# A gated attention and ternary feed-forward block: other places for evictions, and a reordered start-up

## What is computed

```python
x = x + tanh(g_xattn[0]) * attention(layernorm(x), ctx_768, Wq, Wk, Wv, Wo, bo)   # softmax(q k^T / 8) v, then @ Wo + bo
x = x + tanh(g_ffn[0]) * ffn(layernorm(x), w_gate, w_up, w_down)
# ffn: every product is act_quant(h) @ weight_quant(w).T
#   act_quant: rows rounded to 127 steps of their largest magnitude
#   weight_quant: round(w / mean|w|) clipped to -1, 0, 1, times mean|w|
#   h = square(relu(h @ w_gate.T)) * (h @ w_up.T), then @ w_down.T
```

## Time and profile before

| | |
|---|---|
| median of 3 runs | 1192.87 us (1192.4 to 1193.15) |
| the profiled execution | 1192.44 us |
| its span | 1190.6 us |
| TensorE busy | 1170.7 us (98%) |
| VectorE busy | 1034.7 us (87%) |
| ScalarE busy | 870.4 us (73%) |
| GpSimd busy | 300.1 us (25%) |
| mean granted TensorE clock | 0.997 |

### The profile page before, as it was taken

One profiled execution on the slowest core, in us unless ns is written; L12 is line 12 of the kernel. 1 busy time (PEld: TensorE's weight loads), 2 busy tenths in 40 slices (PEclk: granted clock), 3 DMA queues, 4 the chain that ended last, 5 costly groups with the idle time before them and its releaser, 6 DMA issues.

```text
span 1190.6 us, 18823 instructions
## 1 busy us (share of the span) xinstructions
PE 1170.7 (98%) x5851; PEld 740.8 (62%) x5851; DVE 1034.7 (87%) x2124; ACT 870.4 (73%) x929; POOL 300.1 (25%) x301
## 2 busy tenths in 40 slices
PE   9979999999999999999999999999999999999998
PEld 7546656666665666566566656666665666566554
DVE  4988898888988888888998888889899888988887
ACT  5877777776887777677877767776787777677764
POOL 3121222222442222222442222222244222222200
PEclk9999999999999999999999999999999999999999
DMA  9873554443444464444444464443444444444333
GB/s 375 279 255 81 149 145 108 98 110 92 100 115 101 118 164 112 97 106 101 101 99 101 114 172 115 97 110 93 101 112 102 99 97 113 98 105 100 87 66 71
DMA packets 289780, 144.69 MB, mean 122 GB/s; under 512 B 254651, under 2 KB 258063, under 8 KB 287569
## 3 DMA queue, kind: packets, MB, share of 16 engines
q1 hardware_dynamic: 289741, 144.32, 47.4%
q10 hardware_dynamic: 4, 0.00, 0.0%
HBM read 57.86 MB, written 24.35 MB: 69 GB/s over the span
## 4 chain that ended last, share of the span: by engine, by line
PE 87%; DVE 4%; DMA 3%; ACT 2%; SPq 2%; issue 2%; POOL 0%; DVEq 0%; ACTq 0%
PE gu_ps L1110 34%; PE o_ps L1074 18%; PE y_ps L1124 17%; PE s_ps L68 17%; DMA staged<-in_wg_t 2%; SPq L522 1%; DVE half_max L1365 1%; DVE staged L1359 1%; DMA a_scr<-a_spare 1%; DMA hq_t<-staged 0%; PE gu_ps L1243 0%; ACT staged L800 0%; DVE pt_low L1348 0%; PE gu_ps L1212 0%; DVE prob_sum L1341 0%
## 5 line engine op out<-in xcount | busy, mean ns | idle before, releaser
L1110 PE MATMUL gu_ps<-w_up,xq_t 128*128 128x512 bf16 x1024 | 241.9, 379 | 1.9 <-DVE staged L1359 1.8
L1110 PE MATMUL gu_ps<-w_gate,xq_t 128*128 128x512 bf16 x1016 | 240.9, 380 | 1.5 <-DMA xq_t<-xq 1.0
L1124 PE MATMUL y_ps<-w_down,hq_t 128*128 128x512 bf16 x1008 | 228.0, 379 | 0.5 <-DMA hq_t<-staged 0.5
L1074 PE MATMUL o_ps<-v_sb,pt_high 128*128 128x512 f32 (+1 forms) x640 | 214.7, 416 | 6.3 <-DVE pt_low L1348 6.3
L1359 DVE TENSOR_TENSOR staged<-staged,gu_ps 128x1024 f32<-128x1024 f32 x128 | 155.6, 1215 | 54.2 <-ACT staged L806 54.2
L68 PE MATMUL s_ps<-a_sb,xf_high 128*128 128x308 f32 x1024 | 187.4, 305 | 0.0
L1110 PEld LDWEIGHTS gu_ps<-w_up,xq_t 128*128 128x128 bf16 x1024 | 99.8, 98 | 123.8 <-DVE staged L1359 3.8
L846 ACT ACTIVATE staged<-staged,h_scale 128x1024 f32<-128x1024 f32 x126 | 137.9, 1142 | 48.5 <-DVE h_scale L1379 48.5
L1124 PEld LDWEIGHTS y_ps<-w_down,hq_t 128*128 128x128 bf16 x1008 | 98.7, 98 | 119.6 <-DMA hq_t<-staged 1.0
L670 POOL TENSOR_TENSOR rstd<-var_eps,neg_half 128x1 f32<-128x1 f32 x128 | 95.8, 748 | 304.5 <-DVE var_eps L1324 275.6
L800 ACT ACTIVATE staged<-gu_ps 128x1024 f32<-128x1024 f32 x127 | 129.1, 1016 | 52.1 <-PE gu_ps L1110 52.0
(11 more groups left out here) (155 smaller groups left out, 1421.0 us busy)
## 6 DMA issues: line engine op xcount, KB each, us to landing
xf_sb<-in_x_feat SPq DMA_DIRECT2D x64, 256.0 KB, 2.6
x_sb<-in_x_tok SPq DMA_DIRECT2D x64, 256.0 KB, 2.8
y<-staged SPq DMA_DIRECT2D x63, 256.0 KB, 2.1
staged<-in_wg_t SPq DMA_DIRECT2D x4, 1024.0 KB, 18.1
folded<-a_scr SPq DMA_DIRECT2D x3, 1232.0 KB, 6.2
staged<-in_wd_t SPq DMA_DIRECT2D x3, 1024.0 KB, 8.5
folded<-v_scr SPq DMA_DIRECT2D x3, 1024.0 KB, 5.7
w_up<-in_wu_t SPq DMA_DIRECT2D x2, 1024.0 KB, 16.2
```

What stands on the lines that cost most here:

```text
L1074: last = nc.tensor.matmul(o_ps[:, :], pt[0:rows, P * c:P * (c + 1)], v_sb[0:rows, v, c, :], start=(c == 0 and pt is pt_high and v == 0), s ...
L1110: last = nc.tensor.matmul(target[:, q, :], xq_t[:, s.par(0), c, :], w[:, c, cols], start=(c == 0), stop=(c == DC - 1))
L1124: last = nc.tensor.matmul(y_ps[:, :], hq_t[:, c, :], w_down[:, c, :], start=(c == 0), stop=(c == FC - 1))
```

## The change

**Places.** `bo_sb` becomes a buffer of 128 partitions instead of one. The five places of the later values are rows of `x1` (0 to 2), `bo_sb` (3), and the first 512 floats of each partition of `planes_t` (4); all are contiguous rows of 512 floats, and `k_pairs` isn't used for it any more. Parts 0 to 9 go to k mod 5, parts 10 to 15 to places 0, 1, 2, 3, 0, 1. A part waits for the one that had its place: part 14 for part 10, part 15 for part 11. The first turning of planes (tile 1's) waits until place 4 has been stored.

**SyncE's list.** `turn_probs(start, 1)` and `store_keys(3, 2)` go ahead of `store_later_values(11)` and `(12)`.

**ScalarE's list.** `part_probs(start, 1)` goes ahead of `measure(2, 1)`; `measure(2, 3)` leaves ScalarE; `exponentials(start, 2)` goes behind the join and high part of tile 1.

**VectorE's list.** `sum_probs(start, 1)` goes ahead of `ternary(1, 2, w_up)`; `measure(2, 3)` comes in behind `measure(2, 2)`; `probs_low(start, 1)` goes between the two scales; `sum_probs(start, 2)` goes behind `ternary(2, 1, w_down)`; `ternary(2, 0, w_down)` goes into step 0, behind `shift_scores` of tile 3, and there `hidden_half(s, 1)` and `probs_low(s, 2)` go ahead of `top_half(s, 0)` and `ternary(2, 2, w_down)`.

```diff
@@ -39,7 +39,8 @@
 PIECE = WEIGHT // PIECES
 PARTS = PIECE // 512
 A_RING = 2
-V_OUT_RING = 5
+V_PLACES = 5
+V_PLACE = [k % V_PLACES if k < 2 * V_PLACES else (k - 2 * V_PLACES) % (V_PLACES - 1) for k in range(16)]
 FIRST_ROWS = ((BATCH - 1) * KEYS + 1) // 2
 V_LATER = 2 * HEADS
 V_RING = 2
@@ -175,7 +176,7 @@
         v_t = sb("v_t", [P, HP, BATCH * KEYS], F32)
         v_pairs = sb("v_pairs", [P, HP, ALL_KEYS], F32)
         ones = sb("ones", [P, P], F32)
-        bo_sb = sb("bo_sb", [1, DIM], F32)
+        bo_sb = sb("bo_sb", [P, DIM], F32)
         a_spare = sb("a_spare", [P, ALL_KEYS], F32)
         head_mask = sb("head_mask", [P, 2], F32)
         wq_sum = sb("wq_sum", [P, HP], F32)
@@ -198,8 +199,7 @@
         wkv_sb = early[:, 0:2 * CC * INNER].rearrange("p (w c n) -> p w c n", w=2, c=CC)
         ctx_sb = early[:, 2 * CC * INNER:2 * CC * INNER + CC * BATCH * KEYS].rearrange("p (c n) -> p c n", c=CC)
         a_slots = (folded[:, 2 * HP * DIM:2 * HP * DIM + ALL_KEYS], a_spare[:, :])
-        v_slots = [x1[:, 1 + n, :].rearrange("p (q n) -> p q n", q=HP) for n in range(QUAD - 1)]
-        v_slots += [k_pairs[:, :, b, 0:P] for b in range(2)]
+        v_slots = [x1[:, 1 + n, :] for n in range(QUAD - 1)] + [bo_sb[:, :], planes_t[:, :, :].rearrange("p c n -> p (c n)").bitcast(F32)[:, 0:DIM]]
         up_homes = [home[:, :, :].rearrange("p c n -> p (c n)").bitcast(F32) for home in (w_down, w_up)]
         bias_row = centred[0:1, :]
         bias_high = x_marked[0:1, :].bitcast(F32R)
@@ -277,7 +277,7 @@
         a_done, a_taken = sem("a_done"), sem("a_taken")
         vo_done, vo_taken = sem("vo_done"), sem("vo_taken")
         a_stored = [sem(f"a_stored{n}") for n in range(A_RING)]
-        v_stored = [sem(f"v_stored{n}") for n in range(V_OUT_RING)]
+        v_stored = [sem(f"v_stored{n}") for n in range(V_PLACES)]
         a_high_done, a_split_done = sem("a_high_done"), sem("a_split_done")
         xf_high_done, xf_low_done = sem("xf_high_done"), sem("xf_low_done")
         scores_done = sem("scores_done")
@@ -434,8 +434,8 @@
 
                     sp.wait_ge(v_split_done, KC * b)
                     sp.wait_ge(bias_stored, 16)
-                    for n in range(V_OUT_RING):
-                        sp.wait_ge(v_stored[n], 32 * len(range(V_LATER)[n::V_OUT_RING]))
+                    for n in range(V_PLACES):
+                        sp.wait_ge(v_stored[n], 32 * V_PLACE.count(n))
                     full = (KC - 1) * P
                     sp.dma_start(v_raw[:, 0:KC - 1, :], v_scr[b, 0:full, :].rearrange("(c p) n -> p c n", p=P)).then_inc(v_loaded, 16)
                     sp.dma_start(v_raw[0:LAST_ROWS + 1, KC - 1, :], v_scr[b, full:ALL_KEYS + 1, :]).then_inc(v_loaded, 16)
@@ -466,6 +466,9 @@
                     wait(sp, probs_left, s.through(d))
 
                     wait(sp, probs_joined, s.before(d - 1))
+                    if s.opens(1 - d):
+
+                        wait(sp, v_stored[V_PLACES - 1], 32 * V_PLACE.count(V_PLACES - 1))
                     sp.nop(nofuse=True)
                     sp.dma_start_transpose(planes_t[:, :, :], planes[:, :]).then_inc(probs_turned, 16)
 
@@ -519,8 +522,8 @@
                     at = KEYS * head_part(k)[0]
                     sp.wait_ge(vo_taken, k + 1)
                     for b, j, n, r in part_runs(k):
-                        sp.dma_start(v_scr[b, at + j:at + j + n, :].rearrange("p (q n) -> p q n", q=HP),
-                                     v_slots[k % V_OUT_RING][r:r + n, :, :]).then_inc(v_stored[k % V_OUT_RING], 16)
+                        sp.dma_start(v_scr[b, at + j:at + j + n, :],
+                                     v_slots[V_PLACE[k]][r:r + n, :]).then_inc(v_stored[V_PLACE[k]], 16)
 
                 def place_bias():
 
@@ -587,10 +590,10 @@
                 store_later_values(10)
                 store_keys(3, 1)
                 turn_input(start, 0)
+                turn_probs(start, 1)
+                store_keys(3, 2)
                 store_later_values(11)
                 store_later_values(12)
-                turn_probs(start, 1)
-                store_keys(3, 2)
                 store_later_values(13)
                 store_keys(3, 3)
                 store_later_values(14)
@@ -777,11 +780,10 @@
                 def take_later_values(k):
                     rows = head_part(k)[2]
                     act.wait_ge(vo_done, KC + k + 1)
-                    if k >= V_OUT_RING:
-
-                        act.wait_ge(v_stored[k % V_OUT_RING], 32 * (k // V_OUT_RING))
-                    nc.scalar.activation(v_slots[k % V_OUT_RING][0:rows, :, :],
-                                         value_slots[(KC + k) % V_RING][0:rows, :].rearrange("p (q n) -> p q n", q=HP), ACT.Copy,
+                    if k >= V_PLACES:
+
+                        act.wait_ge(v_stored[V_PLACE[k]], 32 * V_PLACE[:k].count(V_PLACE[k]))
+                    nc.scalar.activation(v_slots[V_PLACE[k]][0:rows, :], value_slots[(KC + k) % V_RING][0:rows, :], ACT.Copy,
                                          scale=gate_tanh[0:rows, 0:1]).then_inc(vo_taken, 1)
 
                 def exponentials(s, d):
@@ -897,7 +899,7 @@
                 def gate_bias():
 
                     act.wait_ge(bo_loaded, 16)
-                    nc.scalar.activation(bias_row, bo_sb[:, :], ACT.Copy, scale=gate_tanh[0:1, 0:1]).then_inc(bias_gated, 1)
+                    nc.scalar.activation(bias_row, bo_sb[0:1, :], ACT.Copy, scale=gate_tanh[0:1, 0:1]).then_inc(bias_gated, 1)
                     act.wait_ge(bias_gated, 1)
                     nc.scalar.activation(bias_high, bias_row, ACT.Copy).then_inc(bias_high_done, 1)
 
@@ -969,7 +971,7 @@
 
                 start = Step(act, 0, 0)
                 act.dma_start(gate_row[:, :], gates).then_inc(gates_loaded, 16)
-                act.dma_start(bo_sb[:, :], bo).then_inc(bo_loaded, 16)
+                act.dma_start(bo_sb[0:1, :], bo).then_inc(bo_loaded, 16)
                 take_key_pairs(0)
                 take_key_pairs(1)
                 high_part(start, 0)
@@ -1023,18 +1025,17 @@
                 exponentials(start, 1)
                 take_later_values(11)
                 take_later_values(12)
+                part_probs(start, 1)
                 measure(2, 1)
-                part_probs(start, 1)
                 high_part(start, 3)
                 take_keys(3, 2)
                 take_later_values(13)
-                measure(2, 3)
                 take_keys(3, 3)
                 take_later_values(14)
                 take_later_values(15)
-                exponentials(start, 2)
                 join_probs(start, 1)
                 probs_high(start, 1)
+                exponentials(start, 2)
                 steps_by_batch(act, step, (-1, 0, 1, 2, 3, 4, 5), split_keys, split_values)
 
             @block.tensor
@@ -1387,7 +1388,7 @@
                     for n in range(QUAD - 1):
                         if s.opens(n + 1 - d):
 
-                            wait(dve, v_stored[n], 32 * len(range(V_LATER)[n::V_OUT_RING]))
+                            wait(dve, v_stored[n], 32 * V_PLACE.count(n))
                     here = x1[:, s.ring(d), :]
                     nc.vector.tensor_tensor(here, x_sb[:, s.ring(d), :], o_ps[:, :], ALU.add).then_inc(x1_done, 1)
                     wait(dve, x1_done, s.through(d))
@@ -1571,10 +1572,11 @@
                     top_scores(s, 3)
                     unmark_input(s, 1)
                     shift_scores(s, 3)
+                    ternary(2, 0, w_down)
+                    hidden_half(s, 1)
+                    probs_low(s, 2)
                     top_half(s, 0)
                     ternary(2, 2, w_down)
-                    hidden_half(s, 1)
-                    probs_low(s, 2)
                     ternary(2, 3, w_down)
                     top_half(s, 1)
                     hidden_scales(s)
@@ -1708,11 +1710,12 @@
                 top_scores(start, 1)
                 shift_scores(start, 1)
                 unmark_input(start, 0)
+                sum_probs(start, 1)
                 ternary(1, 2, w_up)
-                sum_probs(start, 1)
                 dve.wait_ge(rstd1_done, 2)
                 input_stats(start, 2)
                 measure(2, 2)
+                measure(2, 3)
                 sum_rows(2)
                 top_scores(start, 2)
                 shift_scores(start, 2)
@@ -1721,11 +1724,10 @@
                 find_unit(2)
                 find_down_unit()
                 scale(2, 0)
-                sum_probs(start, 2)
+                probs_low(start, 1)
                 scale(2, 1)
                 ternary(2, 1, w_down)
-                probs_low(start, 1)
-                ternary(2, 0, w_down)
+                sum_probs(start, 2)
                 steps(dve, step, (-2, -1, 0, 1, 2, 3, 4))
```

## The result

The changed kernel takes 1197.53 us in the median of 6 runs (1197.17 to 1197.89), the kernel before 1192.36 beside it. The ratio is 1.0044, 95% interval 1.0031 to 1.0057: slower by 5.2 us, where 1194.3 within 1189.5 to 1197.0 was forecast. The span of the profiled execution grew from 1190.6 to 1195.8.

A forecast was written before the change was run, and what follows sets the result against it. TensorE ends the chain for 87% of the span, but start-up hangs on VectorE, whose step 0 ends at 111.3 against 109.86: +1.4 us on the 1192.87 median gives 1194.3 us, range 1189.5 to 1197.0.

The forecast's parts named there:

- I take 2.8.: SyncE's store 11, awaited by ScalarE's eviction of part 15: lands 2.8 us after issue, at 80.4, between bounds 2.1 and 4.0.
- So store 11 is issued at 77.2 and 77.6.: SyncE issues store 11 behind the turning (from 73.6) and store_keys(3,2), which waits for ScalarE's take at 76.7.
- rival D: Slower by over 2.4 us through the wait on store 11, with the issue stall kept: 1195.6 to 1196.8, chance 0.22.
- J: Start of ScalarE's join of tile 1's planes: 84.42 before, forecast 81.0, between 80.6 and 82.2.
- SyncE's new wait for place 4 is for store 9, issued by 66: nothing.: SyncE's turning of tile 1's planes waits for store 9 to free place 4; cost taken as nothing.
- E: End of VectorE's step 0: 109.86 before, forecast 111.3, 1.4 us later.
- From J to E: Join to end of VectorE's step 0: J + 30.3, with ScalarE's mark of tile 1's input at J + 16.2.
- The collision: GpSimd's normalise(1) meets a VectorE ternary: normalise takes 2.16 us instead of 1.22, and VectorE loses 0.9.
- The places, and ternary(2,0): Whole-row stores issue in 0.35 us, not 0.88, worth nothing directly; VectorE's ternary adds 1.86 to step 0, otherwise only order changes.
- Rival C: Faster by 3.4 to 5.8 us: the earlier join goes through and TensorE keeps its clock; 1187.1 to 1189.5, chance 0.18.
- The new hole of TensorE: TensorE idles some 6 us before tile 1's gate and up; a clock fall costs up to 2.8 us, hidden behind VectorE.
- VectorE's lag is handed on: VectorE's 1.4 us lag at the end of step 0 passes on, since tile 2's input reached TensorE just in time.

The follow-up runs named there:

- Kernel 2: The changed kernel with part 9 evicted to probs_t, so the turning of tile 1's planes no longer waits for store 9; 1197.32 us, ratio 1.0039.
- Kernel 1: The changed kernel with part 15 evicted to an unused piece of k_pairs, so that eviction no longer waits for store 11; 1195.58 us, ratio 1.0024.
- kernel 3: The changed kernel with parts 15 and 9 both in places of their own, so neither store wait remains; 1195.45 us, ratio 1.0023.
- kernel 9: The changed kernel with sum_probs(1) again behind ternary(1,2) and measure(2,1) again ahead of part_probs(1), all store waits kept; 1197.77 us, ratio 1.0049.
- kernel 10: kernel 3 with sum_probs(1) again behind ternary(1,2) and measure(2,1) again ahead of part_probs(1); 1193.64 us, ratio 1.0012.
- kernel 6: kernel 5 with measure(2,1) again ahead of part_probs(1) on ScalarE and ternary(1,2) again ahead of sum_probs(1) on VectorE; 1190.44 us, ratio 0.9984.
- kernel 12: The kernel before with the change's places alone, every queue in its old order; 1192.53 us, ratio 1.0002.
- kernel 11: kernel 6 with ternary(2,0) moved back out of step 0, behind ternary(2,1) and ahead of step 0; 1191.23 us, ratio 0.9994.
- kernel 8: The kernel before with SyncE's turning and key store ahead of stores 11 and 12, and VectorE's probs_low(1) between the scales; 1192.72 us, ratio 1.0001.
- kernel 5: kernel 3 with exponentials(2) and sum_probs(2) early again, and SyncE's turning of tile 2's planes ahead of the next tile's loads; 1193.34 us, ratio 1.0006.

## Why the prediction was wrong

The price of the wait for store 11 was the step that decided. Two terms of it failed, its issue and its landing; the wait for store 9, put at nothing, is a third, small in what it cost.

**"I take 2.8."** For store 11's landing, from bounds of 2.1 and 4.0. It took 4.69, outside both: 1.9 us. Why is not shown. It is not the size or bulk loads in front alone: the key store issued at 77.89, 1.1 us before it and twice as large, landed after 2.8 (the kernel after, issues of 77.85 to 77.95 us):

```profile
a_scr<-folded SPq DMA_DIRECT2D x1, 308.0 KB, 2.8
```

**"So store 11 is issued at 77.2 and 77.6."** It was issued at 78.61 and 78.95, 1.4 us later. Kernel 2, without the wait for store 9, still issues it at 78.23 and 78.56, since SyncE's stall then falls on the turning (3.37 us to issue). So 0.4 of the 1.4 are the wait for store 9; the rest is that stall, which the sum took as gone and rival D kept, and up to 0.7 of later start (offset), not told apart. The two terms make 1.4 + 1.9 = 3.3 us: the error of J (84.31 against 81.0). So rival D's mechanism decided, with J behind its point of 82.0; its issue times (turning 76.2, store 11 at 78.5 and 78.9) were nearly met, and its upper price, 1196.8, was still too low, because J came at 84.3 and not by 83.5. Kernel 1 measures this wait by itself: 1.9 us of the median, 2.4 by the ratios.

**"SyncE's new wait for place 4 is for store 9, issued by 66: nothing."** The store was issued at 65.86, as the step said, but landed 10.58 us later, behind 2 MB of down weights, a load of features, a key store and store 8 on the same queue. The turning was issued at 76.50 where I had 73.6; in E that cost 0.5 us (kernel 2). A row of the kernel before would have told me: the DMA issues of 63.5 to 64.2 us show a key store, issued at 63.80 behind the same weights and features, landing after 9.1 us.

```profile
a_scr<-folded SPq DMA_DIRECT2D x1, 308.0 KB, 9.1
```

I took "issued long ago" for "landed". That the loads in front are the reason is read off these landings; no run moved them. The Trainium skill's page "SBUF — State Buffer" (The DMA setup-cost knee) fits a transfer's time as 2 us plus its bytes at 436 GB/s, by its figure an estimate of 2.4 us for 154 KB. This trace differs: more than four times that.

**From J to E**, J + 30.3 forecast, J + 30.7 measured. The mark came at J + 16.0 (16.2 forecast) and VectorE stood idle 3.00 in front of it, as said. The ternary in step 0 cost 2.5 instead of 1.9: its first half took 1.86 beside an instruction of GpSimd (102.81 to 104.70), as in the collision that I had priced at the other ternary only. That is 0.6 more, and the rounding came at J + 16.7 instead of 17.0, so part of the closeness is two errors that cancel. This part of the working held, and kernels 1, 2, 3, 9 and 10 keep the same 30.7. The 5.3 us by which this distance grew over the 25.4 of before is what eats the early join; with the earlier sum and the earlier turning it is 26.9 in kernel 6, so 3.8 of them are back.

**The collision.** Forecast 2.16 for normalise(1), measured 2.10; VectorE's idle 0.76 (0.8 forecast), and the ternary's second half took 1.59 us (row 71.59) where the other second halves take 0.69: 0.9 lost, as forecast. Right, but in this kernel free of cost (kernel 9). Once the store waits are gone it seems to count, by 1.3 us (kernel 10, intervals overlapping).

**The places, and ternary(2,0).** Stores of whole rows are issued in 0.3 to 0.4 us instead of 0.88 where there is no stall, worth nothing directly: right (kernel 12). That the ternary's new place changes only the order: right to about 0.6 us of E (kernel 11).

**Rival C** did not come: J was not early. Its condition was tried without the store waits: kernels 1, 3 and 10 attend at 85.48, 84.48 and 83.08, at the full clock, and stay slower than the kernel before, which fits their late sum of tile 2, a condition that C had named. Kernel 8 keeps that sum early, but not the clock, and gains nothing; kernel 6, with both, gains 1.9 us, less than C's 3.4 to 5.8. **The new hole of TensorE** in front of tile 1's gate and up, with the fall of the clock, was forecast (some 6 us) and came: 3.50 us. In the changed kernel the lower clock behind it was hidden, as the forecast said, since the span less E did not grow; in kernel 8 it was not.

**"VectorE's lag is handed on"** was right to a tenth: the span less E did not change.

## What to carry to other kernels

A wait on a store is priced from where the store stands in its queue, not from when it was issued: read the landing time of a transfer issued in the same place, and if bulk loads stand ahead of it, take theirs. Even so it is a bound and not a price: store 11 took longer than the larger store in front of it. When buffers are reused, look at who needs the freed place and what was moved past its store; a store moved behind a turning delays the eviction that needs its place, and through it the very thing that the turning was moved for. And before closing the largest hole of the bottleneck engine, follow the next result that it needs: here the hole moved to the next input until the later sum and the later turning were pulled forward too.

## What was not expected of the hardware

The landing time of stores on SyncE's queue in this stretch goes from 2.8 us (a key store of 308 KB, issued at 77.89) over 4.7 (154 KB, at 78.95) to 10.6 us (154 KB, at 65.86), and not by their size. A stall in issuing is not tied to the kind of store: it fell on k_pairs' store before (5.35), on the turning of the input after (3.75), and on stores 11 and 12 in kernel 12 (4.58 for four issues). And a hole of 2.0 us in front of the same eight folding matmuls left them at 1.31 us in the kernel after, but at 2.26 and 2.42 in kernels 1 and 5; what tells the cases apart stayed open.
